# A pre-norm decoder layer: the order of work inside its attention stage

## The chip, the cores and the metric

One core of one Trainium2 chip runs the whole layer. The metric is the device time of one execution in microseconds (us), as the median of several runs. The engines named here are TensorE (PE in the rows), VectorE (DVE), ScalarE (ACT), GpSimd (POOL) and SyncE (SP), which issues loads and stores.

## The reference, cut to what matters

```python
def attn(h, Wq, bq, Wk, bk, Wv, bv, Wo, bo):        # 16 heads of 32
    q, k, v = (proj(h, W, b) for W, b in ...)       # h @ W.T + b, in heads
    q, k = rope(q), rope(k)
    scores = q @ k.T / sqrt(32)
    # only the first 26 and the last 64 of the 256 keys are seen
    scores = where(key < 26 or key >= 192, scores, -inf)
    out = softmax(scores) @ v
    return out @ Wo.T + bo

x = x + attn(layernorm(x), ...)                     # x: 8 x 256 x 512
x = x + long_conv_gate(ctx, ctx, layernorm(x), ...)
x = x + mixture_of_experts(layernorm(x), ...)       # 12 experts, 3 a token
```

Everything is float32. The change touches the first of the three sums alone.

## The kernel before

The program runs its stages one behind another. `attention` takes the first 318 us, then come `convolution`, a routing stage, `experts` and `finish`, which are the same before and after the change. Each of the five engines has its own instruction queue, written out by hand in the order in which it is to run, and the queues meet in semaphores. So an instruction that waits holds up all that stands behind it on its engine.

`attention` works through 8 batches (B) of 256 tokens, two tiles of 128 tokens each (t = 0, 1). A matrix product with float32 accuracy is made of three products of rounded parts, high by high, high by low, low by high. `three_terms` does so in 12 matmuls of 512 columns for one tile; the four with the low part of the data come last and have a wait of their own (`lo_wait`). The steps of a batch are:

- `normalise` (VectorE) and `x_t` (PE) make the transposed layer-normed tile; `evac_x` (ScalarE) takes its high part and `low_x` (VectorE) its low part out of PSUM.
- `project(b, j)` (PE) makes q of tile 0, q of tile 1, k and v for j = 0 to 3; `add_bias` (VectorE) adds the bias; `rope` (GpSimd, in batch 0 `rope_first` on VectorE) rotates q and k; `qk_t` (PE) transposes them and `evac_q`, `evac_k` (ScalarE) copy them.
- `scores(b, t)` (PE) fills four PSUM banks. `softmax_top` (VectorE) takes the maxima, `exps` (ScalarE) the exponentials and their sums, `softmax_sum` (VectorE) divides, each in two halves of 8 heads.
- `p_t(b, t, half)` (PE) transposes the probabilities into two of the banks of the scores, `evac_pt` (ScalarE) copies them to `pT`, and `p_v` (PE) multiplies by v. `evac_o` and `low_o` split the result, `w_o` (PE) is the output product, and `residual` (VectorE) adds it to x.
- `variance`, `inverse_std`, `normalise_1`, `n_t` and `evac_n` make the second layer norm for the next stage, one batch late.

The batches are software-pipelined: PE's body of batch b holds the projections of batch b + 1. Its order before is scores(b,0), x_t(b+1,1), projections 0 and 1 of b + 1, both p_t of tile 0, projection 2, n_t, scores(b,1), p_v(b,0), qk_t 0, w_o(b,0), qk_t 1, p_t(b,1,0), projection 3, n_t, p_t(b,1,1), qk_t 2, p_v(b,1), x_t(b+2,0), w_o(b,1). Batches 1 to 5 run as a hardware loop, batches 0, 6 and 7 are written out, and batch 7, which has no next batch to prepare, has an order of its own.

The statistics of x for the first layer norm are taken in four parts, of batch 0, of batch 1, of batches 2 and 3, and of batches 4 to 7. The last part stands on VectorE between batch 0 and batch 1 (`stats_of(3)`, `variance_of`), followed by a wait for GpSimd's power of -0.5.

Of the kernel before, what the change touches and what calls it, by code (L numbers as in the profile page):

```python
# [96 lines left out]
def attention(nc, xs, cst, x, wqT, wkT, wvT, woT, bq, bk, bv, bo, consts, qe, taps, diag, kpad):  # L97

    with ExitStack() as ctx:
# [14 lines left out]
        stats = sb("stats", [P, NT, 6])  # L114
        mv = sb("mv", [P, NT, 2])
        rstd = sb("rstd", [P, NT])
# [20 lines left out]
        power = sb("power", [P, NT])  # L137
# [11 lines left out]
        X_PARTS = ((0, 1), (1, 2), (2, 4), (4, B))  # L149
        x_in = [sem(f"x_in{i}") for i in range(len(X_PARTS))]  # L150
        c_in, wq_in, wk_in, wv_in, wo_in, b_in = (sem(n) for n in ("c_in", "wq_in", "wk_in", "wv_in", "wo_in", "b_in"))
# [34 lines left out]

        def t_xt(b, t):
            return (t, 5 + t)[b] if isinstance(b, int) and b < 2 else 7 * b - 4 + t

        def t_qk(b, j):  # L190
            if isinstance(b, int) and b < 2:
                return 5 * b + 2 + j
            return 7 * b + (-1, 0, 2)[j]

        def t_nt(b, t):
            if not isinstance(b, int) or b < B - 2:
                return 7 * b + (12, 15)[t]
            return 7 * B - 4 + 2 * (b - B + 2) + t

        def p_qkv(b, j):
            return 4 + 6 * (b - 1) + (0, 1, 2, 4)[j] if not isinstance(b, int) or b else j

        def p_wo(b, t, last):
            return 4 + 6 * b + (t if last else (3, 5)[t])

        bank_qkv0, bank_qkv, bank_wo, bank_wo_last = (0, 1, 0, 1), (0, 1, 0, 0), (1, 1), (0, 1)

        def key_part(t):  # L210

            return ((0, START, 0), (P - RECENT, P, START))[t]

# [7 lines left out]
        def _(sp):  # L221
# [15 lines left out]
            load_x(1)  # L237
            load_w(WK_, wkT, wk_in)
            load_w(WV_, wvT, wv_in)
            load_w(WO_, woT, wo_in)  # L240
# [7 lines left out]
        def _(act):  # L248
            act.dma_start(cst[:], consts).then_inc(c_in, 16)
            act.wait_ge(c_in, 16)  # L250
            for t, src in ((bias_q, bq), (bias_k, bk), (bias_v, bv), (bias_o, bo)):
# [17 lines left out]
            def evac_x(b, t):  # L269
# [3 lines left out]
                ps = ps_t[:].rearrange("p (k n) -> p k n", k=KD)  # L273
# [33 lines left out]
            def batch(b, late, x_next, last):  # L307
                if not last:
                    evac_x(b + 1, 1)
                exps(b, 0)  # L310
                evac_pt(b, 0)
                if late:
                    evac_n(b - 1)
                evac_o(b, 0)
                if not last:
                    evac_q(b + 1, 0)
                exps(b, 1)
                if not last:
                    evac_q(b + 1, 1)
                evac_pt(b, 1)  # L320
                if not last:
                    evac_k(b + 1)
# [7 lines left out]
            round_w(WK_)  # L330
            evac_q(0, 0)
# [1755 lines left out]
```

## Time and profile before

| | us |
|---|---|
| median of 3 runs | 1538.96 (1538.56 to 1542.29) |
| the profiled execution | 1540.05 |
| its span, first to last instruction | 1538.3 |
| TensorE busy in the span | 1366.7 (89%) |
| attention, 0 to 318.64 us of the span | 318.64 |
| one steady batch of attention | 32.63 |

A busy PE is a PE with a matmul in flight; its matmuls are pipelined, so a matmul of 512 columns shows 0.39 us while the next one starts 0.23 us behind it. In the rows the start of an instruction is therefore of more use than its duration. A merged line such as x4 gives the start of the first and the time to the end of the last.

### The profile page before, as it was taken

Reading aid. Unit: us, or ns where it says so; the run is one execution under the profiler, and the core shown is the slowest. Engines: PE = TensorE matmul, PEld = TensorE weight load, DVE = VectorE, ACT = ScalarE, POOL = GpSimd, SP = SyncE. Lnnn points to the kernel's source line nnn. Section 1 sums busy time; section 2 is a strip of 40 time slices with the busy share of each in tenths; the row PEclk is TensorE's granted clock in tenths of the full one; section 3 lists DMA queues with packets and bytes.
Section 4 is the critical chain, followed back from the end, with each engine's and each line's share of the span. In section 5 each row is a group of like instructions: output and inputs, shape, how many; then the busy total and the mean of one; then the engine's idle time right before and its main releaser. Section 6 shows DMA issues by size and latency. Waiting matters only on the chain. (4 is left out here: it accounts for less than half of the span.)

```text
span 1538.3 us, 27713 instructions
## 1 busy us (share of the span) xinstructions
PE 1366.7 (89%) x7832; PEld 1118.2 (73%) x7833; DVE 818.1 (53%) x1159; ACT 700.2 (46%) x1883; POOL 837.2 (54%) x951
## 2 busy tenths in 40 slices
PE   5879889769998427999999999999999999999974
PEld 3656666557776316888888888888888888888861
DVE  6666766648999697473444717455461644000004
ACT  3445655524465323444444454545454544444530
POOL 0343445134465305767676767677676767565630
PEclk9899999889999658999999999999999999999997
DMA  7000000034333433464443525454462543151116
GB/s 260 1 1 0 0 0 0 1 113 155 96 116 106 150 131 124 117 164 111 107 109 103 144 69 143 120 132 111 118 155 58 156 104 82 34 157 34 35 14 225
DMA packets 75463, 148.23 MB, mean 96 GB/s; under 512 B 9056, under 2 KB 13664, under 8 KB 74912
## 3 DMA queue, kind: packets, MB, share of 16 engines
q1 hardware_dynamic: 60384, 110.89, 23.0%
q0 software_dynamic: 14320, 35.40, 11.5%
q10 hardware_dynamic: 720, 1.45, 0.3%
q8 instruction: 21, 0.34, 0.1%
q14 instruction: 18, 0.15, 0.0%
HBM read 115.11 MB, written 32.59 MB: 96 GB/s over the span
## 5 line engine op out<-in xcount | busy, mean ns | idle before, releaser
L1796 PE MATMUL ps_h<-w_hi,xh 128*128 x708 | 247.2, 361 | 1.5 <-ACT xh L1722 1.4
L1797 PE MATMUL ps_h<-w_lo,xh 128*128 x708 | 242.5, 355 | 0.0
L1819 PE MATMUL ps_y<-w_hi,hh 128*128 x590 | 237.1, 402 | 4.4 <-issue 4.4
L1614 DVE TENSOR_TENSOR w_lo<-stage,w_hi 128x512 f32 x220 | 220.0, 1000 | 28.6 <-DVE w_hi L1612 3.0
L1820 PE MATMUL ps_y<-w_lo,hh 128*128 x590 | 232.1, 393 | 0.0
L1665 POOL TENSOR_TENSOR hl<-h,hh 128x1280 fp32r<-128x1280 f32 x59 | 183.6, 3113 | 16.9 <-ACT hh L1741 16.5
L1675 POOL TENSOR_TENSOR y<-y,b_sb 128x512 f32<-128x512 f32 x58 | 78.7, 1358 | 208.5 <-ACT y L1747 208.5
L1113 PE MATMUL ps_b<-kv,toe 128*128 128x288 f32 x640 | 161.3, 413 | 12.2 <-DMA toe<-kpad 8.7
L1728 ACT ACTIVATE h<-ps_h 128x512 f32<-128x512 f32 x177 | 80.6, 528 | 200.7 <-POOL hl L1665 192.1
L1801 PE MATMUL ps_h<-w_hi,xl 128*128 x708 | 164.7, 355 | 0.0
L1747 ACT ACTIVATE y<-ps_y,wt 128x512 f32<-128x512 f32 x59 | 40.6, 688 | 270.8 <-PE ps_y L1823 270.8
L1737 ACT ACTIVATE h<-ps_td,b_now 128x128 f32<-128x128 f32 x590 | 159.0, 392 | 3.9 <-PE ps_td L1809 1.2
L1113 PEld LDWEIGHTS ps_b<-kv,toe 128*128 128x128 f32 x640 | 122.5, 193 | 47.2 <-DMA toe<-kpad 9.6
L1796 PEld LDWEIGHTS ps_h<-w_hi,xh 128*128 128x128 f32 x708 | 133.6, 189 | 22.3 <-issue 2.1
L1797 PEld LDWEIGHTS ps_h<-w_lo,xh 128*128 128x128 f32 x708 | 133.7, 189 | 20.3
L1612 DVE CAST w_hi<-stage 128x512 f32 x220 | 142.6, 648 | 6.7 <-DMA stage<-in_wcat 6.0
L1823 PE MATMUL ps_y<-w_hi,hl 128*128 x590 | 144.9, 392 | 0.0
L1801 PEld LDWEIGHTS ps_h<-w_hi,xl 128*128 128x128 f32 x708 | 120.4, 189 | 19.2
L1623 DVE TENSOR_TENSOR turn<-wt 128x1 f32<-128x1 f32 x11 | 3.8, 341 | 240.9 <-PE ps_h L1801 240.9
L1819 PEld LDWEIGHTS ps_y<-w_hi,hh 128*128 128x128 f32 x590 | 111.5, 189 | 26.8 <-issue 4.6
L1823 PEld LDWEIGHTS ps_y<-w_hi,hl 128*128 128x128 f32 x590 | 110.8, 188 | 24.4
L1820 PEld LDWEIGHTS ps_y<-w_lo,hh 128*128 128x128 f32 x590 | 111.6, 189 | 22.6
(246 smaller groups left out, 2431.3 us busy)
## 6 DMA issues: line engine op xcount, KB each, us to landing
stage<-in_wcat SPq DMA_DIRECT2D x220, 256.0 KB, 2.9
toe<-kpad SPq DMA_DIRECT2D x32, 256.0 KB, 3.3
cc<-in_ctx_rev SPq DMA_DIRECT2D x32, 192.0 KB, 3.3
w_lo<-in_wcat SPq DMA_DIRECT2D x4, 1280.0 KB, 10.1
acc<-added_c POOLq DMA_DIRECT2D x1, 4352.0 KB, 16.7
x2d<-xs SPq DMA_DIRECT2D x16, 256.0 KB, 2.4
xnd<-xn_c SPq DMA_DIRECT2D x16, 256.0 KB, 2.1
w_hi<-x2d SPq DMA_DIRECT2D x2, 2048.0 KB, 12.9
```

The costliest lines, as they stand in the source:

```text
L1113: last = nc.tensor.matmul(view(ps[:], (4 * par + l) * 512, [[SPAN, B], [1, NPAIR]]), toe[:, par, (l - m) * P:(l - m + 1) * P], kv[:, buf, ...
L1612: nc.vector.tensor_copy(hi, stage[:, c % NSTAGE]).then_inc(w_rounded, 1)
L1614: nc.vector.tensor_tensor(lo, stage[:, c % NSTAGE], hi.bitcast(F32), ALU.subtract).then_inc(split_done, 1)
L1665: nc.gpsimd.tensor_tensor(hl[:], h[:], hh[:].bitcast(F32), ALU.subtract).then_inc(hl_ready, 1)
L1728: nc.scalar.activation(h[:, lo:hi], ps_h[:, c, 0:hi - lo], ACT.Copy).then_inc(h_evac, 1)
L1737: last = nc.scalar.activation(h[:, k * P:(k + 1) * P], ps_t[:, k // 4, (k % 4) * P:(k % 4 + 1) * P], ACT.Relu, bias=b1_now[:, k:k + 1])
L1796: nc.tensor.matmul(out, x_hi, part(w_hi, e, k * FF + lo, hi - lo), start=(k == 0), stop=False)
L1797: nc.tensor.matmul(out, x_hi, part(w_lo, e, k * FF + lo, hi - lo), start=False, stop=False)
L1801: last = nc.tensor.matmul(out, xl[:, k * P:(k + 1) * P], part(w_hi, e, k * FF + lo, hi - lo), start=False, stop=(k == KD - 1))
L1819: nc.tensor.matmul(ps_y[:], h_hi, part(w_hi, e, KD * FF + k * D, D), start=(k == 0), stop=False)
L1820: nc.tensor.matmul(ps_y[:], h_hi, part(w_lo, e, KD * FF + k * D, D), start=False, stop=False)
L1823: last = nc.tensor.matmul(ps_y[:], hl[:, k * P:(k + 1) * P], part(w_hi, e, KD * FF + k * D, D), start=False, stop=(k == KF - 1))
```

## The change

Six things are changed, all inside `attention`.

1. PE's order in a batch becomes: w_o(b-1,1), x_t(b+1,1), projections 0 and 1 of b + 1, both p_t of tile 0, n_t, scores(b,1), projection 2, p_v(b,0), qk_t 0, projection 3, p_t(b,1,0), n_t, p_t(b,1,1), qk_t 1, w_o(b,0), qk_t 2, p_v(b,1), scores(b+1,0), x_t(b+2,0). So the next batch's first scores run ahead of this batch's second output product.
2. VectorE and ScalarE follow. VectorE takes the second `low_o` and `residual` of a batch between the two halves of the next batch's `softmax_top`. ScalarE puts `evac_x(b+1,1)` between the two halves of `exps(b,0)`, and the exponentials of tile 1 ahead of `evac_o(b,0)`.
3. Statistics of x are taken for one batch (two tiles) at a time, inside batch b for batch b + 3, and GpSimd's power likewise.
4. Loads: x of batch 1 is loaded behind the weights of k and v, x of batch 2 alone, x of batches 3 to 7 last. The biases of v and of the output are loaded behind the rounding of the k weights.
5. In the beginning the tile x_t(0,1) goes to a bank of its own, the weights of k are split right behind those of q, all three rotations come ahead of the split of v, and projection 3 of batch 0 comes behind scores(0,0).
6. In batch 7, w_o(6,1) comes behind scores(7,0), and VectorE's maxima and sums of the two tiles are interleaved.

```diff
             load_w(WK_, wkT, wk_in)
             load_w(WV_, wvT, wv_in)
+            load_x(1)
             load_w(WO_, woT, wo_in)
...
@@ ScalarE
-            def batch(b, late, x_next, last):
-                if not last:
-                    evac_x(b + 1, 1)
-                exps(b, 0)
+            def batch(b, late, x_next):
+                exps(b, 0, (0,))
+                evac_x(b + 1, 1)
+                exps(b, 0, (1,))
                 evac_pt(b, 0)
                 if late:
                     evac_n(b - 1)
+                exps(b, 1)
+                evac_q(b + 1, 0)
                 evac_o(b, 0)
...
                 evac_pt(b, 1)
+                evac_q(b + 1, 1)
+                evac_k(b + 1)
                 evac_o(b, 1)
                 if x_next:
                     evac_x(b + 2, 0)
...
+            for t, src in ((bias_v, bv), (bias_o, bo)):
+                act.dma_start(t[:], src.partition_broadcast(P)).then_inc(bvo_in, 16)
+            round_w(WV_)
             evac_q(0, 0)
...
@@ VectorE, a batch b > 0 of the new order
+                add_bias(b, 3)
+                softmax_top(b, 0, steps, (0,))
+                low_o(b - 1, 1)
+                low_x(b + 1, 0)
+                softmax_top(b, 0, steps, (1,))
+                residual(b - 1, 1, steps)
+                low_x(b + 1, 1)
+                softmax_sum(b, 0, steps, (0,))
+                variance(b - 1)
+                softmax_sum(b, 0, steps, (1,))
+                add_bias(b + 1, 0)
+                normalise_1(b - 1)
+                add_bias(b + 1, 1)
+                softmax_top(b, 1, steps)
+                add_bias(b + 1, 2)
+                normalise(b + 2, 0)
+                stats_of(b + 3, 0)
+                normalise(b + 2, 1)
+                softmax_sum(b, 1, steps)
+                evac_n(b - 1)
+                stats_of(b + 3, 1)
+                low_o(b, 0)
+                variance_of(b + 3)
+                residual(b, 0, steps)
...
@@ VectorE, between batch 0 and the loop
-            stats_of(3)
-            variance_of(4 * TPB, NT)
-            dve.wait_ge(std_ready, 4)
-            with dve.Fori(1, B - 2) as b:
+            with dve.Fori(1, B - 3) as b:
...
@@ PE
+                w_o(b - 1, 1)
+                x_t(b + 1, 1)
+                project(b + 1, 0)
+                project(b + 1, 1)
                 p_t(b, 0, 0)
                 p_t(b, 0, 1)
                 n_t(b - 1, 0)
                 scores(b, 1)
+                project(b + 1, 2)
                 p_v(b, 0)
+                qk_t(b + 1, 0)
+                project(b + 1, 3)
                 p_t(b, 1, 0)
                 n_t(b - 1, 1)
                 p_t(b, 1, 1)
+                qk_t(b + 1, 1)
+                w_o(b, 0)
+                qk_t(b + 1, 2)
                 p_v(b, 1)
+                scores(b + 1, 0)
                 x_t(b + 2, 0)
...
@@ PE, ahead of batch 0
-            project(0, 2, bank_qkv0[2])
-            qk_t(0, 0)
-            project(0, 3, bank_qkv0[3])
-            qk_t(0, 1)
-            qk_t(0, 2)
+            for j in range(3):
+                project(0, j)
+            for j in range(3):
+                qk_t(0, j)
+            scores(0, 0)
+            project(0, 3)
+            x_t(1, 0)
```

(The conditions for the first and last batches are left out of the two bodies above. In batch 0 the new body of VectorE has the bias of v, the split of the output weights and the statistics of batch 2 in it as well.)

## Rows read from the trace of the kernel before

**Rows 1.** The page, busy time of each engine (us, share of span, instructions).
```profile
PE 1366.7 (89%) x7832; PEld 1118.2 (73%) x7833; DVE 818.1 (53%) x1159; ACT 700.2 (46%) x1883; POOL 837.2 (54%) x951
```

**Rows 2.** Windows by stage: length, each engine's busy us, clock, DMA share, GB/s.
```profile
0.00:79.79 79.79, 53.15 (x356) 39.93 (x358) 48.22 (x92) 31.16 (x96) 16.55 (x25) 0.89 0.35 126
79.79:120.09 40.30, 30.76 (x265) 23.27 (x261) 28.35 (x61) 19.08 (x78) 16.61 (x17) 0.92 0.00 1
...
152.72:185.35 32.63, 29.10 (x264) 22.37 (x260) 22.67 (x44) 19.09 (x78) 14.96 (x16) 1.00 0.00 0
...
250.62:279.11 28.49, 24.46 (x216) 18.83 (x213) 19.48 (x38) 18.22 (x76) 15.48 (x16) 1.00 0.00 1
279.11:318.64 39.53, 25.04 (x212) 19.39 (x212) 22.84 (x48) 14.27 (x70) 1.40 (x2) 0.77 0.00 1
```

**Rows 3.** PE's timeline in a steady batch: start, duration, line, idle before and releaser.
```profile
150.63 1.09 PE L687 MATMUL bank<-wo_hi,oT_lo 128*128 128x512 f32 x4
151.65 1.14 PE L717 MATMUL bank<-kT,qT 32*128 32x90 f32 x32
...
153.13 0.48 PE L683 MATMUL bank<-wq_hi,xT_hi 128*128 128x512 f32 x1
...
159.57 1.08 PE L725 MATMUL bank<-cst,pm 128*90 128x128 f32 x8 [0.59 <-DVE pm L510]
161.56 1.07 PE L725 MATMUL bank<-cst,pm 128*90 128x128 f32 x8 [0.92 <-DVE pm L510]
162.39 0.47 PE L683 MATMUL bank<-wk_hi,xkT_hi 128*90 128x512 f32 x1
...
165.28 0.60 PE L661 MATMUL bank<-cst,xn 128*128 128x128 f32 x4
...
173.03 1.07 PE L725 MATMUL bank<-cst,pm 128*90 128x128 f32 x8 [0.80 <-DVE pm L510]
...
178.98 0.53 PE L661 MATMUL bank<-cst,qkb 90*128 90x90 f32 x4 [0.78 <-DVE qe L541]
...
181.33 0.47 PE L683 MATMUL bank<-wo_hi,oT_hi 128*128 128x512 f32 x1 [0.22 <-ACT oT_hi L305]
```

**Rows 4.** VectorE's timeline at the next batch's start.
```profile
184.39 0.69 DVE L516 TENSOR_TENSOR yo<-bank,bias_o 128x512 f32<-128x512 f32 x1 [1.60 <-PE bank L687]
...
186.63 0.89 DVE L500 TENSOR_REDUCE mx<-bank 128x8 f32<-128x720 f32 x1
...
188.69 0.42 DVE L467 TENSOR_TENSOR xkT_lo<-bank,xkT_hi 128x256 fp32r<-128x256 f32 x1
...
189.63 0.99 DVE L438 TENSOR_SCALAR xn<-xs,mv,rstd 128x512 f32 x2
...
191.23 0.91 DVE L510 TENSOR_TENSOR pm<-pm,rden 128x720 f32<-128x720 f32 x1
```

**Rows 5.** ScalarE's timeline in the same steady batch, the two copies of `pT`.
```profile
160.68 1.02 ACT L296 ACTIVATE pT<-bank 90x1024 f32<-90x1024 f32 x1 [0.35 <-PE bank L725]
162.67 1.02 ACT L296 ACTIVATE pT<-bank 90x1024 f32<-90x1024 f32 x1 [0.97 <-PE bank L725]
```

**Rows 6.** Timelines of VectorE, then GpSimd, then PE around 80 to 92 us.
```profile
80.96 4.83 DVE L421 BATCH_NORM_STATS2 stats<-xs 128x6 f32<-128x512 f32 x8
...
86.81 1.65 POOL L400 TENSOR_TENSOR rstd<-rstd,power 128x8 f32<-128x8 f32 x1 [17.29 <-DVE rstd L428]
...
91.86 2.08 PE L687 MATMUL bank<-wq_hi,xT_lo 128*128 128x512 f32 x4 [6.74 <-DVE xT_lo L469]
```

**Rows 7.** Timelines of VectorE, then PE, in the first 60 us.
```profile
27.98 2.36 DVE L459 TENSOR_TENSOR wv_lo<-qe,wv_hi 128x1024 fp32r<-128x1024 f32 x2 [1.46 <-ACT wv_hi L266]
...
37.42 2.03 PE L717 MATMUL bank<-kT,qT 32*128 32x90 f32 x32 [1.65 <-ACT kT L259]
...
54.24 3.51 PE L725 MATMUL bank<-cst,pm 128*90 128x128 f32 x16 [3.14 <-DVE pm L510]
```

**Rows 8.** PE's timeline in the last batch.
```profile
296.57 1.93 PE L741 MATMUL bank<-pT,vv 90*32 90x128 f32 x32 [1.21 <-issue]
```

More of the change, by code:

```diff
@@ L563, in batch @@
-                if late:
-                    normalise_1(b - 1)
-                if not last:
-                    add_bias(b + 1, 2, bank_qkv[2])
-                softmax_top(b, 1, steps)
-                low_o(b, 0)
-                softmax_sum(b, 1, steps)
-                residual(b, 0, last, steps)
-                if late:
-                    evac_n(b - 1)
-                if not last:
-                    add_bias(b + 1, 3, bank_qkv[3])
-                low_o(b, 1)
-                if x_next:
-                    low_x(b + 2, 0)
@@ L578, in batch @@
-                residual(b, 1, last, steps)
-            stats_of(0)
-            variance_of(0, TPB)
-            dve.wait_ge(std_ready, 1)
+                softmax_sum(b, 1, steps)
+                if not first:
+                    evac_n(b - 1)
+                if more:
+                    stats_of(b + 3, 1)
+                low_o(b, 0)
+                if more:
+                    variance_of(b + 3)
+                residual(b, 0, steps)
+            stats_of(0, 0)
+            stats_of(0, 1)
@@ L626, in _ @@
             b = B - 1
-            softmax_top(b, 0, tail)
-            softmax_top(b, 1, tail, 0)
+            add_bias(b, 3)
+            softmax_top(b, 0, tail, (0,))
+            low_o(b - 1, 1)
+            softmax_top(b, 0, tail, (1,))
+            residual(b - 1, 1, tail)
+            softmax_sum(b, 0, tail, (0,))
+            softmax_top(b, 1, tail, (0,), 0)
+            softmax_sum(b, 0, tail, (1,))
+            softmax_top(b, 1, tail, (1,), 0)
             variance(b - 1)
-            softmax_sum(b, 0, tail)
             softmax_sum(b, 1, tail, (0,))
@@ L652, in free_t, with free_p, transposes @@
                     pe.wait_ge(t_evac, idx)
-            def free_p(idx):
-                if not isinstance(idx, int) or idx > 1:
-                    pe.wait_ge(p_evac, idx - 1)
-            def transposes(idx, done, src, rows):
-                free_t(idx)
+            def free_p(before):
+                if before is not None:
+                    pe.wait_ge(p_evac, before + 1)
+            def transposes(done, src, rows, out):
                 for k in range(KD):
-                    last = nc.tensor.transpose(ps_t[:, k * P:k * P + rows], src[0:rows, k * P:(k + 1) * P],
+                    last = nc.tensor.transpose(out[:, k * P:k * P + rows], src[0:rows, k * P:(k + 1) * P],
                                                ident[0:rows, 0:rows])
@@ L743, in p_v, with batch @@
                 last.then_inc(pv_done, 1)
-            def batch(b, late, x_next, last):
-                scores(b, 0)
-                if isinstance(b, int) and b == 0:
-                    x_t(1, 0)
-                if not last:
-                    x_t(b + 1, 1)
-                    project(b + 1, 0, bank_qkv[0])
-                    project(b + 1, 1, bank_qkv[1])
+            def batch(b, late, x_next):
+                if late:
+                    w_o(b - 1, 1)
+                x_t(b + 1, 1)
+                project(b + 1, 0)
+                project(b + 1, 1)
                 p_t(b, 0, 0)
                 p_t(b, 0, 1)
-                if not last:
-                    project(b + 1, 2, bank_qkv[2])
                 if late:
@@ L813, in _ @@
             p_v(b, 1, True)
[L814 removed]
+            w_o(b, 1)
             n_t(b, 0)
```

280 lines of the change are left out of this document (142 added, 138 removed).

## The prediction

> **What bounds the kernel now.** I read the page first, then windows cut by stage, then PE's timeline of one batch, and the other engines only where PE waited. The page gives PE 89% of the span, far above any other engine [rows 1], so time is won where PE stands still or runs at half clock. The change is inside attention, the first 318.64 us, so I cut windows there at each start of the transposes x_t(b+1,1), a place that both orders have with the same work done before it [rows 2]. The reader is to see four stretches: a beginning of 79.79 us with PE busy for 53.15, a batch 1 of 40.30, steady batches of 32.63 (batches 2 to 5, four of them, all alike), and an end of 28.49 + 39.53.
>
> In a steady batch PE is busy 29.10 of 32.63 us, VectorE 22.67, ScalarE 19.09, GpSimd 14.96, the granted clock 1.00 (the 2.4 GHz level) [rows 2]. PE is idle for the rest, 3.53 us, at six waits: both p_t of tile 0 wait for VectorE's quotients (0.59, 0.92), w_o twice for ScalarE's high part (0.22 each), p_t(b,1,0) for a quotient 0.80, and the transposes of k 0.78 for a copy by VectorE [rows 3]. Each wait costs a little more than its idle time: a new group starts about 0.16 us ahead of the drain of the one before where nothing waits: the products of 2.89 hold 12 matmuls at 0.24, and the last four with their drain show 1.09 and not 0.96. So 3.53 + 6 x 0.16 = 4.5 us of a batch are lost, and 28.1 us are work. No engine but PE is near 28.
>
> **The steady batch, step by step.** Nothing is taken out of PE's queue, so its 28.1 us stay. The lengths, start to start: a product of 12 matmuls 2.89 (165.28 - 162.39), half a tile of p_t 0.83, scores and a tile transpose together 1.48 [rows 3]. VectorE: a residual 2.24, half a softmax_top 1.03 (188.69 - 186.63 is two), low_x 0.94, the quotient of a half about 1.05 with its reciprocal (0.91 shown) [rows 4]. ScalarE: eight exponentials 2.50, one copy of pT 1.02 [rows 5]. I count from the start of w_o(b-1,1).
>
> - w_o(b-1,1) at 0. Its high part was made while scores(b,0) and x_t ran (1.48 us), so that wait goes. Its low part is wanted at 8 x 0.24 (2.89 / 12) = 1.9. VectorE comes from residual(b-1,0) and the bias of v at about 0.1, does half a softmax_top to 1.1 and low_o to 1.7. It arrives 0.1 to 0.2 ahead, which is the thinnest place of the new order.
> - x_t(b+1,1) 2.9, projections 3.3 and 6.2, end 9.0. VectorE: low_x 2.6, second half of the top 3.6, residual 5.9 (w_o's end was needed at about 3.1), low_x 6.8, first quotient 7.9; ScalarE has had the first exponentials by 3.7 and the second by 7.0, second quotient by 9.4. p_t(b,0,0) is wanted at 9.0, p_t(b,0,1) at 9.9: the two waits of 0.59 and 0.92 go.
> - n_t at 10.7, then scores(b,1) at 11.2. In the old order projection 2 lay in front of these scores; it is moved behind them. They need both copies of pT: the first starts 1.11 behind its p_t (160.68 - 159.57), the second follows it, so they end at 9.0 + 1.11 + 2 x 0.97 = 12.1 [rows 3, 5]. A new wait of 0.95 us.
> - projection 2, p_v, transposes of q, projection 3 from 13.2 to 20.5. VectorE's tops of tile 1 at 13.3 to 15.8, exponentials to 19.6, bias, two normalises and one new statistics instruction in between, first quotient by 20.1, second by 21.2; p_t wanted at 20.5 and 21.8. The wait of 0.80 goes with 0.4 us of slack.
> - The transposes of q of tile 1 wait for evac_n behind n_t, some 0.15. They no longer wait 0.78. Then w_o(b,0), whose inputs have long been there, the transposes of k, whose rotation (GpSimd, 14.96 us in all) ends 1.3 before, p_v, scores(b+1,0), x_t, and the batch closes.
>
> Lost before 4.5, lost now 0.95 + 0.15, and I add 0.15 for the thin place: 28.1 + 1.25 = 29.4 us. A steady batch gains 3.2. The statistics moved in (two instructions of 0.6 each by 4.83 / 8, a short variance of about 0.5) make VectorE 22.67 + 1.7 = 24.4 us of 29.4, hidden beside PE [rows 2, 6]; if that cover went it would be 1.7 us a batch. Bounds of a batch: 29.0 with no slack lost, 30.8 if GpSimd's rotation stretches VectorE's work so that quotients and low_o come some 0.5 late at three places.
>
> **Batch 1.** It lasts 40.30. Behind batch 0 VectorE takes eight tiles' statistics (4.83) and GpSimd a power over eight columns (1.65), and only then come the maxima; the low part of x is late and PE stands for 6.74 us in the middle of a projection, then runs at half clock (four matmuls in 2.08, against 1.09) [rows 3, 6]. With two tiles a batch this block is gone and batch 1 is like the others: 40.30 - 29.4 = 10.9. The four others: 4 x 3.23 = 12.9.
>
> **The beginning.** The old scores(0,0) start at 37.42, behind a split of the v weights (27.98, 2.36 long) that itself waited for ScalarE, behind projection 3, and behind the rounding of the output weights [rows 7]. The new order asks for none of these. Projections 0 to 2 run back to back, ending near 21.5; VectorE does three additions and rotations of about 2.9 each from near 17.7 to 26.4, the transposes and a copy follow, and scores(0,0) start near 27.6 (bounds 26.5 to 31, the upper if the k weights land no earlier). PE has waited before that, and I take half clock (matmuls 0.43 apart, from 2.08 for four with their drain) for scores, projection 3 and projection 0 of batch 1: 2.0 + 5.1, transposes of both tiles with a high and a low part between them to 38.1, 5.1 and 2.8, so p_t(0,0,0) at 46.0 instead of 54.24 [rows 7]. From there the same work up to the mark is 20.9 us at full clock, 0.95 for the copies of pT, and 1.9 because the split of the output weights now lies ahead of tile 1's quotients; the mark comes at about 70, 9.7 earlier than 79.79. I take 9.0; bounds 5 (clock low for twice as long) to 12.
>
> **The end.** From x_t(7,1) (250.62) to the last batch's first p_v (296.57) it is 45.95 us [rows 2, 8]. New: 25.0 to scores(7,0), by the steady batch. Then, from there: half a top by 2.6, low_o 3.2, half a top 4.2, w_o(6,1) ends by 4.3, residual 6.7, quotient 7.7, top 8.7, exponentials of half a tile 11.2, two copies of pT 13.1, p_v at 13.1. Together 38.1, a gain of 7.8 (bounds 4 to 10). What follows is as before.
>
> **The sum.** 9.0 + 10.9 + 12.9 + 7.8 = 40.6. Against its own execution, 1540.05 (span 1538.3 and 1.75 around it), that makes 1499.5; the median of the runs shown, 1538.96, lies 1.1 below that execution, so 1498.4. I say 1499. The loads and biases that are reordered are priced in the beginning alone: all land before 30 us and nothing behind the first batch waits for them.
>
> A rule that could speak against it: the clock. In this trace the steady batches kept 1.00 through six waits a batch, and the stage at the end, with PE busy 25.04 of 39.53 us, shows 0.77 [rows 2]. The Trainium skill, "TensorE: Matmul & The Clock Gate" (Part 1), says the same in kind, that PE is passed at 1.2 or 2.4 GHz by how busy it has lately been. By that rule a fuller PE should keep its clock in the batches and win a little more in the end than I take; the beginning, where the new order leaves PE idle ahead of scores(0,0), could run low for longer.
>
> **Rivals.**
> - *The beginning and the end hardly gain* (chance 0.15): the chain there is VectorE's own, the PE stands anyway, and the clock is half in between. For: clock 0.89 and 0.77 there. Against: rotations and maxima truly come sooner. 2 + 10.9 + 12.9 + 3 = 28.8: 1510.
> - *VectorE becomes the bound in the batches* (0.14): low_o and the quotients come late behind the moved residual, batch 31.5. For: 0.1 us of slack at low_o, and GpSimd runs beside VectorE. Against: 24.4 of 29.4 us. 9 + 8.8 + 4 x 1.1 + 6 = 28.2: 1511.
> - *The batches lose their clock* (0.05): if the one wait of 0.95 let it fall to the mean of the old batch 1, 0.92, some 8% of 28.1 us go in each, 5 x 2.2 = 11: 1510. Against: waits of 0.92 left it at 1.00 [rows 2, 3].
> - *Slower* (0.03): the ring low_o, w_o, residual, quotients, p_t, maxima, low_o. If each turn waits for the one before, PE's period is VectorE's and ScalarE's chain. It decides once a batch exceeds 29.4 + 40.6 / 6 = 36.2 us, that is, low_o 6.8 us late. At 38 us a batch: 6 x 8.6 = 52 less 40.6, 1550. Nothing in the rows is that long.
> - *No change* (0.02): the block at batch 1 is only moved and paid elsewhere, and the new waits eat the rest.
>
> The forecast itself has 0.61, with its own range of 1493 to 1505. With the rivals at 1510 the range is 1491 to 1512. About 0.3% (4.6 us) is what a measurement of this kernel tells from no change. Faster 0.95, same 0.02, slower 0.03.
>
> **What would show it.** Right: windows cut at x_t(b+1,1) of 29 to 30 us for batches 1 to 5, all alike, clock 1.00; one PE wait of about 0.8 before scores(b,1) for ScalarE's pT, no waits for quotients; scores(0,0) near 28, the first p_t near 46, attention's end near 278. Wrong: PE idle before the last four matmuls of w_o(b-1,1) (low_o late), idle before p_t with VectorE named, or a first mark beyond 75.

## The result and the profile after

The changed kernel takes 1498.88 us (median of 4 runs, 1498.71 to 1499.93), against 1540.62 for the kernel before on the same chip (median of 4, 1538.56 to 1543.89). The ratio is 0.9734, with a 95% interval of 0.9712 to 0.9756. The profiled execution of the changed kernel took 1498.73 us, with a span of 1497.0. The prediction was 1499.

The page of the changed kernel, busy time of each engine, answers to [rows 1]:

```profile
PE 1355.4 (91%) x7832; PEld 1115.5 (75%) x7833; DVE 822.0 (55%) x1167; ACT 699.8 (47%) x1883; POOL 841.7 (56%) x955
```

TensorE has the same 7832 matmuls. It is busy for 11.3 us less, and the other 30 us of the 41.3 that the span lost were idle time. The 11.3 are not all clock: in the steady batches, at 1.00 before and after, PE is busy 0.8 us less a batch (28.30 against 29.10), which fits the 0.16 of drain that a wait adds to the busy time in front of it, as several waits are gone. VectorE has 8 instructions more, the finer statistics.

The windows, cut at the starts of x_t(b+1,1) as in [rows 2] (length, busy us of each engine, clock, DMA share, GB/s):

```profile
0.00:70.25 70.25, 49.06 (x357) 37.77 (x359) 50.78 (x94) 33.30 (x109) 20.51 (x26) 0.93 0.39 143
70.25:99.45 29.20, 28.34 (x262) 22.55 (x261) 24.64 (x50) 18.97 (x80) 15.96 (x17) 1.00 0.01 2
99.45:128.61 29.16, 28.30 (x261) 22.55 (x260) 24.71 (x50) 18.96 (x80) 15.95 (x17) 1.00 0.00 0
...
186.94:215.79 28.85, 28.14 (x262) 22.56 (x261) 22.62 (x44) 18.89 (x80) 15.24 (x16) 1.00 0.00 0
215.79:240.18 24.39, 23.68 (x214) 18.84 (x212) 16.97 (x33) 15.64 (x65) 15.12 (x16) 1.00 0.00 1
```

The reader is to see that the second row, batch 1, is now like the third, where before it was 40.30 against 32.63. PE is busy 28.3 of 29.2 us, and VectorE 24.7 where it was 22.67. The fourth row, batch 5, has no statistics left to take. The convolution's first matmul starts at 281.13 us instead of 324.31, so attention lost 43.18 us. The unchanged rest took 1215.87 us instead of 1213.99. This rest scatters between 1213.9 and 1217.2 in the profiles of this study, so small differences between kernels are read below from the end of attention, and from single batches.

PE's timeline of the changed kernel over one batch, answering to [rows 3] (start, duration, line; in brackets the idle time before and what ended it):

```profile
95.77 0.66 PE L699 MATMUL bank<-cst,xn 128*128 128x128 f32 x4
96.55 0.49 PE L725 MATMUL bank<-wo_hi,oT_hi 128*128 128x512 f32 x1
...
98.51 1.09 PE L729 MATMUL bank<-wo_hi,oT_lo 128*128 128x512 f32 x4
...
105.45 1.91 PE L766 MATMUL bank<-cst,pm 128*90 128x128 f32 x16
107.20 0.60 PE L699 MATMUL bank<-cst,xn 128*128 128x128 f32 x4
108.51 1.14 PE L758 MATMUL bank<-kT,qT 32*128 32x90 f32 x32 [0.71 <-ACT pT L327]
...
116.79 1.03 PE L766 MATMUL bank<-cst,pm 128*90 128x128 f32 x8
117.67 0.60 PE L699 MATMUL bank<-cst,xn 128*128 128x128 f32 x4
118.10 1.04 PE L766 MATMUL bank<-cst,pm 128*90 128x128 f32 x8
119.17 0.66 PE L699 MATMUL bank<-cst,qkb 128*128 128x128 f32 x4
```

All the quotient waits of [rows 3] are gone: the 16 matmuls of tile 0's p_t run as one group, and those of tile 1 follow the product of v at once. One wait is left with a mark, 0.71 before scores(b,1) for ScalarE's copy of pT. Two small ones carry no mark and are seen only in the starts. From 118.10 to 119.17 it is 1.07 where the half before it took 0.88, so 0.19 is lost. From x_t to w_o, 95.77 to 96.55, it is 0.78 where x_t takes some 0.40 elsewhere, so 0.38 is lost. With the 0.88 before scores(b,1), 1.31 from 107.20 to 108.51 less 0.43 for n_t, that is 1.45 us a batch.

VectorE in the same batch, answering to [rows 4]:

```profile
95.73 0.67 DVE L482 TENSOR_TENSOR vv<-bank,bias_v 90x512 f32<-90x512 f32 x1
...
97.37 0.69 DVE L503 TENSOR_TENSOR oT_lo<-bank,oT_hi 128x512 fp32r<-128x512 f32 x1
...
113.22 0.66 DVE L468 TENSOR_SCALAR xn<-xs,mv,rstd 128x512 f32 x1
...
114.40 0.53 DVE L468 TENSOR_SCALAR xn<-xs,mv,rstd 128x512 f32 x1
...
115.07 1.34 DVE L540 TENSOR_TENSOR pm<-pm,rden 128x720 f32<-128x720 f32 x1
```

The low part of the output (97.37 + 0.69 = 98.06) is there 0.45 us before its matmuls want it at 98.51. The first quotient of tile 1 ends at 116.41, 0.38 before p_t at 116.79. The addition of the bias of v, the first row, ends at 96.40, just before w_o starts at 96.55.

The beginning and the end on PE, answering to [rows 7] and [rows 8]:

```profile
29.16 2.03 PE L758 MATMUL bank<-kT,qT 32*128 32x90 f32 x32 [0.56 <-ACT kT L290]
...
43.56 1.91 PE L766 MATMUL bank<-cst,pm 128*90 128x128 f32 x16
46.61 1.14 PE L758 MATMUL bank<-kT,qT 32*128 32x90 f32 x32 [1.15 <-ACT pT L327]
...
57.58 3.55 PE L766 MATMUL bank<-cst,pm 128*90 128x128 f32 x16 [2.51 <-DVE pm L540]
...
253.78 1.08 PE L782 MATMUL bank<-pT,vv 90*32 90x128 f32 x32 [1.57 <-issue]
```

The first scores start at 29.16 (before 37.42), the first p_t at 43.56 (before 54.24), and the last batch's first p_v at 253.78 (before 296.57). At 57.58 stands the one large wait that the change left in batch 0, with half clock behind it: 16 matmuls in 3.55 us, against 1.91.

### The profile page after: what moved, and what is told of

It is laid out like the page before. It is cut to its first block and busy times, and to the rows that moved or that the text cites. A ratio compares the mean times of both kernels' runs of the same rounds, so it can differ in the third digit from the quotient of the medians.

```text
span 1497.0 us, 27687 instructions
## 1 busy us (share of the span) xinstructions
PE 1355.4 (91%) x7832; PEld 1115.5 (75%) x7833; DVE 822.0 (55%) x1167; ACT 699.8 (47%) x1883; POOL 841.7 (56%) x955
## 3 DMA queue, kind: packets, MB, share of 16 engines
q10 hardware_dynamic: 720, 1.45, 0.3%
## 5 line engine op out<-in xcount | busy, mean ns | idle before, releaser
L1781 ACT ACTIVATE y<-ps_y,wt 128x512 f32<-128x512 f32 x59 | 40.6, 688 | 272.3 <-PE ps_y L1857 272.3
L1646 DVE CAST w_hi<-stage 128x512 f32 x220 | 137.9, 627 | 5.0 <-DMA stage<-in_wcat 4.5
L1857 PEld LDWEIGHTS ps_y<-w_hi,hl 128*128 128x128 f32 x590 | 110.8, 188 | 24.4
```

The costliest lines, as they stand in the source:

```text
L1646: nc.vector.tensor_copy(hi, stage[:, c % NSTAGE]).then_inc(w_rounded, 1)
L1857: last = nc.tensor.matmul(ps_y[:], hl[:, k * P:(k + 1) * P], part(w_hi, e, KD * FF + k * D, D), start=False, stop=(k == KF - 1))
```

## The experiments

Each kernel is the changed one with one edit or a few, but for the first, which is the kernel before with one part of the change. "Mark" is the start of x_t(2,1), the end of the beginning, 70.25 in the changed kernel; x_t(1,1) starts at 37.51 there. Windows and rows are of one profiled execution each, which need not be the median one.

### The statistics alone, in the kernel before

```diff
-            stats_of(3)
-            variance_of(4 * TPB, NT)
-            dve.wait_ge(std_ready, 4)
+            # in batch b: stats_of(b + 3, 0), stats_of(b + 3, 1), variance_of(b + 3)
```

> The kernel before with one part of the change alone: statistics of x for two tiles a batch, taken inside batch b for batch b + 3, GpSimd's power likewise; every other queue in the old order. My theory (the block of eight tiles between batch 0 and batch 1 was worth about what a batch lasted over 32.63): windows cut at x_t(b+1,1) give 32.6 to 33.2 us for batch 1 instead of 40.30, the other batches stay at 32.6 since the new instructions lie in VectorE's idle time, and batch 0 gains 1 to 2 us; in all 8 to 9.5 us less than before, 1531 to 1533. Rival (the old order has no room for them, the gain of batch 1 needs the new order): batches of 33.6 or more, in all under 4 us less.

Measured: 1533.67 against 1539.37, ratio 0.9956 (0.9939 to 0.9974). Batch 1 is 33.14 long instead of 40.30, a gain of 7.2, and the mark is at 76.58 instead of 79.79: from x_t(1,1) to it there are 33.79 us instead of 37.23, so batch 0 gains 3.4 more. The other batches grew from 32.63 to 33.2. Attention ends 10.7 us earlier in the profile. The medians show only 5.7; this kernel's runs lie between 1528.11 and 1535.22, and the profiled one, 1529.98, is among the short ones. What follows: the block of batch 1 was as dear as the walk had it, 7.2 of batch 1's gain of 11.1 being its own, and in the old order the added VectorE work was not hidden. It cost 0.6 us a batch, mostly as a wait for low_o that the batch before did not have, next to the old ones of [rows 3]:

```profile
161.48 1.20 PE L693 MATMUL bank<-wo_hi,oT_lo 128*128 128x512 f32 x4 [0.44 <-DVE oT_lo L476]
```

### The output product ahead of the next scores again

```diff
@@ PE
                 w_o(b - 1, 1)
+                scores(b, 0)
                 x_t(b + 1, 1)
...
                 p_v(b, 1)
-                scores(b + 1, 0)
                 x_t(b + 2, 0)
@@ VectorE
+                low_o(b - 1, 1)
+                low_x(b + 1, 0)
                 softmax_top(b, 0, steps, (0,))
-                low_o(b - 1, 1)
-                low_x(b + 1, 0)
                 softmax_top(b, 0, steps, (1,))
```

> The changed kernel with one part undone: the next batch's first scores run behind the second output product again, and VectorE's second low_o in front of the first softmax_top, as it then must be. My theory: w_o(b-1,1) waits 0.4 us again for its high part, the first quotients come 0.4 late, the second 0.9, so a steady batch lasts about 31.0 instead of 29.16, in all 10 to 12 us more than the changed kernel, 1509 to 1511. Rival (VectorE and ScalarE have so much room now that this order does not matter): under 0.5 us a batch, 1499 to 1502.

The last batch has the old order in the same way. Measured: 1518.65, ratio 0.9872 (0.9855 to 0.9888); batches of 32.36, 3.2 longer than in the changed kernel, and 4.6 us more from x_t(7,1) to the convolution (69.95 against 65.34). Both are more than I had expected. PE's waits in one of its batches, then the window of it:

```profile
138.64 0.47 PE L725 MATMUL bank<-wq_hi,xT_hi 128*128 128x512 f32 x1 [1.41 <-ACT xT_hi L306]
144.55 1.14 PE L758 MATMUL bank<-kT,qT 32*128 32x90 f32 x32 [0.50 <-ACT pT L327]
162.10 0.50 PE L725 MATMUL bank<-wo_hi,oT_hi 128*128 128x512 f32 x1 [1.19 <-DVE vv L482]
```

```profile
133.79:166.16 32.37, 29.15 (x264) 22.24 (x261) 25.72 (x49) 18.84 (x78) 15.92 (x17) 1.00 0.00 0
```

The largest wait, 1.41, is one that I had not seen: ScalarE has the copy of the next tile behind the first half of the exponentials, and these start only when the scores, now late, are there. The third, 1.19, is the w_o at the head of the batch, which wants the bank that VectorE empties when it adds the bias of v. With the scores ahead this addition is done beside them. So this swap of scores and w_o, with all else in the new order, is worth nearly as much as the steady batch gained in all (3.5 us). The granted clock stayed at 1.00 through these waits.

### Projection 2 ahead of the second scores again

```diff
@@ PE
                 p_t(b, 0, 1)
+                project(b + 1, 2)
                 n_t(b - 1, 0)
                 scores(b, 1)
-                project(b + 1, 2)
@@ VectorE
-                softmax_top(b, 1, steps)
                 add_bias(b + 1, 2)
+                softmax_top(b, 1, steps)
```

> The changed kernel with one move undone: projection 2 of the next batch in front of scores(b,1) again, with its bias in front of the maxima of tile 1. My theory: the wait of 0.71 idle (0.95 by starts) before scores(b,1) goes, but these scores run about 1.9 us later and so do maxima, exponentials and quotients, and p_t(b,1,0) then waits about 2.5: a batch 30.5 to 30.9 instead of 29.16, in all 8 to 11 us more than the changed kernel, about 1508. Rival (the second half of a batch has slack, only the wait counts): 28.3 us a batch, 1493.

Measured: 1521.09, ratio 0.9887 (0.987 to 0.9903). Four batches of 34.15, and 31.16 for batch 5. The profiled execution took 1528.56, the longest of five; the other four lie between 1520.07 and 1521.74, so these batches may not be those of a typical execution. Here the expectation failed, which had 30.5 to 30.9 a batch. A wait in a steady batch of it, then the windows of a batch with statistics and of batch 5, without:

```profile
159.96 1.94 PE L766 MATMUL bank<-cst,pm 128*90 128x128 f32 x8 [3.03 <-DVE pm L540]
```

```profile
140.33:174.47 34.14, 30.99 (x261) 25.11 (x260) 25.50 (x50) 19.09 (x80) 15.88 (x17) 0.90 0.00 0
...
208.59:239.75 31.16, 28.43 (x262) 22.51 (x261) 23.40 (x44) 18.83 (x80) 15.30 (x16) 1.00 0.00 0
```

The wait of 0.88 before scores(b,1) is gone, and one of 3.03 has come before p_t(b,1,0). The way from scores(b,1) over two maxima, two halves of exponentials and a quotient to p_t is longer than the work that PE has in between, so every microsecond by which these scores start later comes back there. And PE's clock falls to its 1.2 GHz level behind the wait: 8 matmuls in 1.94 us, against 1.03. By the busy times that is 30.99 - 28.30 = 2.7 us more. Together 29.16 - 0.88 + 3.03 + 0.16 + 2.69 = 34.16, which is the batch as measured. In batch 5, which has no statistics, PE waits 1.76 there and then 0.37 and 0.59 behind it, and the clock stays at 1.00. So the new wait of 0.88 that the change brought is the cheap side of this choice.

### Loads and biases as before

```diff
+            load_x(1)
             load_w(WK_, wkT, wk_in)
             load_w(WV_, wvT, wv_in)
-            load_x(1)
...
-            for t, src in ((bias_q, bq), (bias_k, bk)):
+            for t, src in ((bias_q, bq), (bias_k, bk), (bias_v, bv), (bias_o, bo)):
```

> The changed kernel with the old loads: x of batch 1 ahead of the k weights, all four biases at once. My theory: the k weights' rounding starts about 1.0 us later (16.6 instead of 15.6), the chain on VectorE up to scores(0,0) moves by that, and nothing else: the mark x_t(2,1) at 71.2 instead of 70.25, in all 0.5 to 1.5 us more, 1499.5 to 1500.5. Rival (the beginning was bound by loads): 3 us or more, scores(0,0) at 32 or later.

Measured: 1503.33 (1499.13 to 1506.45), ratio 0.9777 (0.9755 to 0.9799). In the profile the mark is at 70.54 (70.25), and attention ends at 280.84 (281.13): no difference there. The medians lie 4.5 us apart, but the intervals overlap, and the beginning itself scatters. In kernels with the new loads ScalarE's rounding of the k weights starts at 15.62 (changed kernel), 14.48 (the same kernel run again, mark 68.48), 14.43, 12.90 and 12.62. With the old order of the loads it starts at 16.65 in this kernel, at 16.60 in the kernel before and at 17.64 in that with the statistics alone. The first row is of this kernel, the others are the latest and the earliest with the new order:

```profile
16.65 2.01 ACT L297 ACTIVATE wk_hi<-qe 128x1024 fp32r<-128x1024 f32 x2 [4.62 <-DMA qe<-in_L_attn_Wk]
```

```profile
15.62 1.06 ACT L297 ACTIVATE wk_hi<-qe 128x1024 fp32r<-128x1024 f32 x1 [3.30 <-DMA qe<-in_L_attn_Wk]
```

```profile
12.62 1.06 ACT L297 ACTIVATE wk_hi<-qe 128x1024 fp32r<-128x1024 f32 x1 [0.47 <-DMA qe<-in_L_attn_Wk]
```

So the weights of k land earlier with the new order in every profile, by 1.0 to 5.0 us. What comes of it in the time is left open: the mark of kernels with an unchanged beginning is at 70.25, 68.48 and 68.41 with the new loads and at 70.54 with the old, some 0.3 to 2 us.

### Half of projection 2 ahead of the second scores

The wait is 0.88 by the starts, and four matmuls 0.23 apart cover it, so the product is cut in two.

```diff
                 n_t(b - 1, 0)
+                project2_head(b + 1)   # 4 matmuls of 12
                 scores(b, 1)
-                project(b + 1, 2)
+                project2_rest(b + 1)   # the other 8
```

> The changed kernel with projection 2 of the next batch cut in two on PE: its first 4 of 12 matmuls run in front of scores(b,1), in the place of the new wait (0.71 idle, 0.87 by starts), the other 8 behind. My theory: the wait is gone, but the quotients of tile 1 are ready only 0.3 us before p_t(b,1,0) wants them, since two normalises and a statistics instruction lie in front of them on VectorE, so most of the gain turns into a wait there: a batch 28.7 to 28.9 us instead of 29.16. Rival (a PE wait removed is a PE wait gained): 28.3 us a batch.

Measured twice: 1496.81, ratio 0.9734 (0.9705 to 0.9763); batches of 28.90 and a last one of 28.32. The wait for pT is gone, and one for the quotient has come:

```profile
112.49 1.08 PE L788 MATMUL bank<-cst,pm 128*90 128x128 f32 x8 [0.26 <-DVE pm L540]
```

A batch gains 0.27 of the 0.88. The new wait takes 0.26 + 0.16 of it back: the experiment with projection 2 in small. The remaining 0.2 are not traced to one place.

### The same, with the first quotient ahead of the normalises

```diff
+                softmax_sum(b, 1, steps, (0,))
                 normalise(b + 2, 0)
                 stats_of(b + 3, 0)
+                softmax_sum(b, 1, steps, (1,))
                 normalise(b + 2, 1)
-                softmax_sum(b, 1, steps)
```

> As the kernel with the cut projection 2, and VectorE's quotient of the first half of tile 1 is put in front of the normalise and the statistics instruction, the second normalise behind the second half. My theory: now the whole 0.87 us is kept, a batch 28.3 to 28.5 us. Rival (exponentials on ScalarE are the limit, not VectorE's order): the same 28.7 to 28.9 as without this order.

Measured: 1503.14, ratio 0.9772 (0.9738 to 0.9806); batches of 30.34, and one of 31.87. The theory fell. PE's waits in one batch, then VectorE beside them:

```profile
117.07 1.07 PE L789 MATMUL bank<-cst,pm 128*90 128x128 f32 x8 [0.91 <-DVE pm L540]
118.97 0.66 PE L700 MATMUL bank<-cst,qkb 128*128 128x128 f32 x4 [0.83 <-DVE qe L569]
```

```profile
113.86 1.07 DVE L468 TENSOR_SCALAR xn<-xs,mv,rstd 128x512 f32 x1
...
116.94 1.38 DVE L468 TENSOR_SCALAR xn<-xs,mv,rstd 128x512 f32 x1
```

The first quotient was in time, but it had to wait for the exponentials, and VectorE stood. The normalises behind it ran 1.07 and 1.38 us, where the changed kernel shows 0.66 and 0.53. So the second quotient and `evac_n` were late instead. Both kernels have these normalises beside a rotation of GpSimd, only beside other instructions of it, so why they stretch more here is not shown.

The batch of 31.87 is the third. It has the same two waits, 0.90 and 0.83, but its matmuls behind the second are 0.43 apart up to 152.65, and its window shows a clock of 0.95 where the other batches show 1.00:

```profile
128.41:160.28 31.87, 30.02 (x262) 23.71 (x261) 25.30 (x50) 19.00 (x80) 15.84 (x17) 0.95 0.00 0
```

### The beginning: the output weights split behind the quotients

```diff
-                if first:
-                    split_w(WO_)
                 normalise(b + 2, 0)
...
                 softmax_sum(b, 1, steps)
+                if first:
+                    split_w(WO_)
...
+            add_bias(0, 0)      # was the first of those behind the split
             split_w(WK_)
```

> The changed kernel with two edits in the beginning: VectorE splits the output weights behind both quotients of tile 1 of batch 0 and not in front of them, and adds the bias of projection 0 in front of the split of the k weights, while it waits for them. My theory: PE's wait of 2.51 before p_t(0,1,0) goes and with it the half clock behind it (p_t at 3.55 for 16), and scores(0,0) start 0.6 earlier; the mark x_t(2,1) at 65.5 to 67 instead of 70.25, in all about 4 us less. Rival (w_o(0,0) then waits for its weights for as long): mark at 69 or later.

Measured: 1497.09, ratio 0.9742 (0.9717 to 0.9767); mark 68.01, end of attention 279.17. From x_t(1,1) to x_t(2,0) it is 27.86 us, against 29.18 in the changed kernel: 1.3 less, where the wait and the half clock that were to go come to 4. PE's waits of this kernel in batch 0, then VectorE's split:

```profile
54.59 1.08 PE L768 MATMUL bank<-cst,pm 128*90 128x128 f32 x8 [0.18 <-DVE pm L540]
56.07 1.07 PE L768 MATMUL bank<-cst,pm 128*90 128x128 f32 x8 [0.40 <-DVE pm L540]
57.84 0.47 PE L727 MATMUL bank<-wo_hi,oT_hi 128*128 128x512 f32 x1 [0.26 <-DVE wo_lo L489]
59.44 0.50 PE L727 MATMUL bank<-wo_hi,oT_hi 128*128 128x512 f32 x1 [0.44 <-DVE wo_lo L489]
...
62.17 0.53 PE L701 MATMUL bank<-cst,qkb 90*128 90x90 f32 x4 [0.34 <-POOL qkb L404]
```

```profile
55.93 3.45 DVE L489 TENSOR_TENSOR wo_lo<-qe,wo_hi 128x1024 fp32r<-128x1024 f32 x2
```

The wait of 2.51 and the half clock behind it are gone, so the cause of both was the split. It then took 3.45 us instead of the 2.35 it took in the changed kernel, and five smaller waits came in its place, the last for GpSimd's rotation of k. The split has two-input work of GpSimd beside it in both kernels. In the changed one it kept its 2.35, and GpSimd's instruction, begun before it, gave way; here both were longer. The two in the changed kernel:

```profile
51.34 2.35 DVE L489 TENSOR_TENSOR wo_lo<-qe,wo_hi 128x1024 fp32r<-128x1024 f32 x2
...
51.00 3.33 POOL L401 TENSOR_TENSOR rs<-qkb,cst 128x256 f32<-128x256 f32 x1
```

### The output product at the end of the loop's body

```diff
             def batch(b, late, x_next):
-                w_o(b - 1, 1)
                 x_t(b + 1, 1)
...
                 x_t(b + 2, 0)
+                w_o(b, 1)
```

> The changed kernel with the edge of PE's hardware loop moved: the body ends with w_o(b,1) instead of beginning with w_o(b-1,1), the order of all matmuls is the same. In batches inside the loop 0.78 us lie between x_t(b+2,0) and w_o(b,1), where 4 transposes take about 0.42. My theory (the jump back costs some 0.3 us where little work is queued in front of it, and nothing behind 12 long matmuls): batches 1 to 4 at 28.85 as the one outside the loop shows, in all 1.2 us less. Rival (w_o waits there for its bank or its high part): 29.16 as before.

Measured twice: 1498.78, ratio 0.9747 (0.9717 to 0.9777); batches of 29.10, attention's end at 281.29 (281.13). The order of the work is the same, only the jump of the loop lies elsewhere, and x_t to w_o is still 0.69 (0.78). So nearly all of the 0.38 us before w_o(b-1,1) is not the jump's. The weight load ahead of the product in this kernel names the cause:

```profile
94.62 0.19 PEld L725 LDWEIGHTS bank<-wo_hi,oT_hi 128*128 128x128 f32 x1 [0.27 <-DVE vv L482]
```

It is the PSUM bank of the v projection: VectorE adds the bias of v behind residual(b,0), and w_o(b,1) goes into that bank. In the changed kernel this addition ends at 96.40, and w_o starts at 96.55.

The expectation took batch 5 (28.85) for one outside PE's loop. That is wrong: on PE it is in the loop, and only VectorE has it written out. By the starts its 0.31 us lie at two places, 0.12 at the transposes of q (205.60 to 206.55, against 118.10 to 119.17) and 0.20 before w_o, which stands 0.57 behind x_t at 212.32 and not 0.78:

```profile
212.89 0.50 PE L725 MATMUL bank<-wo_hi,oT_hi 128*128 128x512 f32 x1
```

Both places wait for VectorE.

### The normalises last

```diff
-                normalise(b + 2, 0)
+                softmax_sum(b, 1, steps, (0,))
                 stats_of(b + 3, 0)
-                normalise(b + 2, 1)
-                softmax_sum(b, 1, steps)
+                softmax_sum(b, 1, steps, (1,))
                 evac_n(b - 1)
+                normalise(b + 2, 0)
+                normalise(b + 2, 1)
```

With the split of projection 2 as well.

> The changed kernel with projection 2 cut 4 + 8 around scores(b,1), and on VectorE the two normalises of tile 1's stretch put behind evac_n, so that in front of the quotients stand no instructions that GpSimd stretches (a normalise took 0.5 us alone and up to 1.38 beside a rotation). My theory: the first quotient follows its exponentials, the second too, evac_n comes in time, and a batch lasts 28.4 to 28.7 us instead of 29.16: 3 to 4.5 us in all. Rival (PE's ring over VectorE, from w_o(b,0) by the residual to the bias of v and w_o(b,1), takes it back): 28.9 or more.

Measured: 1496.85 (1496.19 to 1497.22), ratio 0.9721 (0.9706 to 0.9736). The batches took 29.65 to 29.70, so the theory fell for them: the wait has moved on to low_o.

```profile
115.69 1.08 PE L788 MATMUL bank<-cst,pm 128*90 128x128 f32 x8 [0.21 <-DVE pm L540]
119.89 1.20 PE L729 MATMUL bank<-wo_hi,oT_lo 128*128 128x512 f32 x4 [0.81 <-DVE oT_lo L503]
```

What it lost in the batches it had gained in the beginning, where it took 27.5 us from x_t(1,1) to x_t(2,0).

### All of these together

The split of projection 2, the order just shown and the new beginning.

> The last kernel with the two edits in the beginning as well (output weights split behind the quotients of batch 0, first bias in front of the split of the k weights). My theory: from x_t(1,1) to x_t(2,0) 27.9 us instead of 29.2, batches of 28.4 to 28.7, in all 4 to 6 us less than the changed kernel, 1493 to 1495. Rival (what is won in attention is lost in the spread of the later stages, so that medians do not tell them apart): within 3 us of it.

Measured: 1502.5, ratio 0.9757 (0.9741 to 0.9772), 5.0 above the changed kernel that was measured beside it (next section); mark 74.10, attention's end at 287.38 against 281.02.

```profile
62.99 2.07 PE L731 MATMUL bank<-wo_hi,oT_lo 128*128 128x512 f32 x4 [2.27 <-DVE oT_lo L503]
```

In batch 0 the split of the output weights (3.44) and both normalises (2.35) now stand ahead of low_o, and each part alone had left it room.

### The changed kernel again

> The changed kernel itself, as a yardstick on this chip. Both theories: median 1497 to 1502; batches of 29.16; the beginning up to the mark x_t(2,1) between 66.5 and 70.5, by when the k weights land (their rounding began at 15.62 in one profile and at 12.6 to 14.4 in kernels with the same loads).

Measured: 1497.45 (1496.71 to 1502.28), ratio 0.9733 (0.9714 to 0.9752). Batches of 29.17, attention's end at 281.02. Four of its five executions lie below 1498.1, the fifth is the one at 1502.28. Of the two kernels measured beside it as often, the one at 1496.85 is not told from it. The one at 1502.5 has a median 5.0 longer and an attention 6.4 longer, so I call it slower, though the intervals of the ratios overlap.

### A wait of a size between

Projection 2 ahead of scores(b,1) as above, with VectorE's order of the normalises last: a shorter wait than 3.03 at the same place.

> Projection 2 in front of scores(b,1), as in the kernel whose batches lasted 34.15 us with a PE wait of 3.03 and half clock behind it, but with VectorE's quotients ahead of the normalises, so that the wait is about 2.0. My theory: the clock stays at 1.00 in the batches and a batch lasts 30.3 to 31.2, that is, the half clock was 2.7 of the 5 us. Rival (the clock falls with this place of the wait, not with its length): clock 0.9 again and 33 us or more.

Measured twice: 1515.28, ratio 0.9841 (0.9818 to 0.9863). Batches of 32.46, 31.36, 31.35, 32.66 and 30.95. The windows of the second and the fourth, and the fourth's waits:

```profile
103.33:134.69 31.36, 28.50 (x262) 22.51 (x261) 24.17 (x50) 18.91 (x80) 15.81 (x17) 1.00 0.00 0
...
166.04:198.70 32.66, 29.91 (x262) 23.76 (x261) 24.15 (x50) 18.91 (x80) 15.79 (x17) 0.95 0.00 0
```

```profile
184.37 1.08 PE L766 MATMUL bank<-cst,pm 128*90 128x128 f32 x8 [1.75 <-DVE pm L540]
...
187.07 1.94 PE L766 MATMUL bank<-cst,pm 128*90 128x128 f32 x8 [0.33 <-DVE pm L540]
```

Every batch has a wait of about 1.75 (1.55 in the last) and one of 0.56 behind it, and in four of the five a third of 0.3 to 0.4. The clock kept 1.00 in three of five batches and fell in two, at a price of 1.1 and 1.3 us. So the length of the wait is not all that decides; what does, these runs don't show.

## Why the prediction was right

It was right in its mechanism and in most of its steps. That the time came within 0.2 us is luck. The forecast sum was 40.6, and attention lost 43.2: 9.54 in the beginning, 11.10 in batch 1, 14.19 in the four others, 7.96 up to the last batch's first p_v and 0.39 behind it. The unchanged rest took 1.9 us more in the same execution, which is scatter, and that hid most of the difference of 2.6. Inside the batch and inside the beginning errors cancelled as well.

- *What bounds the kernel.* That PE's idle time and half clock are what counts holds: the 43.18 us of attention came with the same matmuls.
- *The steady batch*, 29.4 forecast, 29.16 measured. The waits for quotients and for ScalarE's high part went, as said. The wait before scores(b,1) was forecast at 0.95 and is 0.88. That of the transposes of q was forecast at 0.15 and is 0.19.
- *The thin place.* I added 0.15 for w_o's low part, which was to arrive 0.1 to 0.2 ahead. It arrived 0.45 ahead and cost nothing. But w_o itself starts 0.38 late, for the bank that VectorE empties with the bias of v. I had walked the data that w_o needs and not the bank that it writes; this is the step that failed. It is the same ring (residual, bias of v, w_o), one link further on. The two belong together: without the 0.38 w_o would want its low part at 98.13, and it is there at 98.06, so the place is as thin as forecast and the wait for the bank covers it.
- *The work of a batch.* The waits now come to 0.88 + 0.19 + 0.38 = 1.45, against my 1.25, so the work is 27.7 and not 28.1. I had priced only the six marked waits of the old batch at 0.16 each and counted all else as work. Group by group against the changed kernel's starts the 0.4 is no one hidden wait: it is spread over some ten places with 0.1 or less at each, the largest the 0.10 before each w_o.
- *VectorE*, 24.4 forecast, 24.7 measured, and hidden. The experiment with the statistics alone shows that this held for the new order only: in the old one they cost 0.6 a batch.
- *Batch 1*, 10.9 forecast, 11.10 measured; batches 2 to 5, 12.9 and 14.19, which is most of what attention won beyond the forecast.
- *The beginning*, 9.7 walked and 9.0 taken, 9.54 measured, again a sum of two errors. The first scores came at 29.16 and not at 27.6. The first p_t came at 43.56 and not 46.0 all the same, because the clock was full from 33.71 on (matmuls 0.23 apart): projection 3 took 4.0 and projection 0 of batch 1 2.86, where I had 5.1 for each; projection 1 I had at full clock already. What was won there was lost at 57.58: I had priced the split of the output weights at 1.9, and it cost 2.51 + 0.16 of wait and 1.6 of half clock.
- *The end*, 38.1 forecast from x_t(7,1) to the first p_v, 37.99 measured (253.78 - 215.79), of which 24.4 to scores(7,0) for 25.0 and 13.6 behind it for 13.1. Attention's end was to be near 278. By the same point, VectorE's last copy, it is 275.46 instead of 318.64.
- *The rivals.* VectorE as the bound of the batches did not come, but it is close: it appears as soon as 0.88 us are taken from PE. The clock as the price of a wait is real, at 3.03 us, sometimes at 1.75, and once in four batches with waits of 0.90 and 0.83. The changed order's batches have one marked wait of 0.71, and there it stayed at 1.00. Long waits for quotients exist: in the experiment with projection 2 first they made a batch 34.15 long, short of the 36.2 at which the gain would have been lost.

Which part bought what, from the experiments: the statistics 7.2 us in batch 1 and 3.4 in batch 0, measured in the old order, where they cost 0.6 in each later batch; the swap of scores and w_o 3.2 a batch and 4.6 in the last; scores(b,1) ahead of projection 2 another 5 a batch against the order without it, in an execution longer than the others of that kernel. The last two can't be added, because each is measured with the other in place. The order of the loads lets the weights of k land earlier, with no clear gain in time. The beginning's other edits (item 5) and the interleaved maxima of batch 7 (item 6) were not taken apart.

## What to carry to other kernels

Walk the bounding engine's queue from start to start and follow for each group the data it reads, the bank it writes and what stands ahead on the engine that releases it. The walk of data gave 29.4 for 29.16; what it missed in the new order was a bank, 0.38 us. Once PE is busy 28.3 of 29.2 us and the next engine 24.7, taking away PE's last wait returns as another: of six attempts here none is faster than the changed kernel by more than the intervals, and the one that joined three of them was slower than it. When a wait must stand somewhere, put it where it is short and the chain behind it long: 0.88 us before the scores saved 3.03 before their transposes, and the half clock behind that.

## What the runs showed of the hardware

- A wait of 3.03 us in an otherwise dense PE cost 5.9 us in each of four batches: 3.19 itself and 2.7 of half clock behind it. With 1.75 and 0.56 in one batch both outcomes occurred, two batches in five at the lower clock.
- Below 3.03 the length of a wait did not decide. Waits of 1.41, 0.50 and 1.19 in every batch left the clock at 1.00 in the kernel with the output product first, while 0.90 and 0.83 brought it down in one batch of four in the kernel with the split and the quotient first (31.87 against 30.34).
- VectorE's instructions on SBUF stretch beside GpSimd's rotation, by much and by place. The normalise took 0.52 to 1.38 us, the quotient 0.91 to 1.64, a split of two weight halves 2.35 to 3.45. The two quotients of tile 0, at 103.15 and 104.65 us, kept 0.91: GpSimd was idle up to 104.57, and then busy with a power over two columns. The Trainium skill, "SBUF — State Buffer" (SBUF: two separate sides), says that VectorE and GpSimd share a pair of ports, claimed by VectorE's faster mode or its work with two SBUF inputs, and that the one that starts first has it for its whole instruction while the other waits. The rows agree that the two hold each other up, but not on who waits. GpSimd's instruction at 51.00, 0.75 elsewhere, took 3.33 and ended behind the split that began 0.34 after it and kept its 2.35. And the quotient at 104.65 kept its 0.91 although the power had begun 0.08 before it.
- The rounding that waits for the first k weights started between 12.62 and 15.62 us in eleven profiles with the same loads in the same order, and x_t(1,1) between 33.90 and 37.71.
- The batches in VectorE's hardware loop take 29.16 us, and batch 5, written out on VectorE and without statistics, takes 28.85. VectorE stands idle before its copy `evac_n` in both. In the loop that copy starts 0.15 behind the end of n_t (117.67 + 0.60 to 118.42), written out 0.04 (205.16 + 0.60 to 205.80). So this 0.11 is not the time of the statistics' instructions; what in the loop it is was not tested.
